# A mixture-of-experts tile stage with gate and up computed as features by tokens

## The reference

```python
router_logits = x @ gate_w.T                       # 16 experts
topk_w, topk_idx = top_k(softmax(router_logits), 4)  # 4 experts per token, weights normalised
shared = (silu(x @ Wg.T) * (x @ Wu.T)) @ shared_down.T * sigmoid(x @ shared_gate_vec.T)
for each expert e:                                 # 176 inner features
    h = silu(x @ gate_e.T) * (x @ up_e.T)
    acc = acc + (h @ down_e.T) * combine[:, e]
out = x + shared + acc
```

## Time and profile before

| what | value |
|---|---|
| median of 3 runs | 620.12 us (616.87 to 622.4) |
| profiled execution, its own time | 620.9 us |
| its span, first to last instruction | 619.1 us |
| mean granted TensorE clock | 0.986 of 2.4 GHz |
| TensorE matmul busy | 582.2 us (94%) |
| TensorE weight load busy | 457.3 us (74%) |
| VectorE busy | 492.9 us (80%) |
| ScalarE busy | 415.8 us (67%) |
| GpSimd busy | 396.7 us (64%) |

### The profile page before, as it was taken

How to read it: one execution, slowest core, us unless ns; L and a number is a source line. 1 busy time by engine, 2 the same in 40 slices (tenths; PEclk the granted TensorE clock), 3 DMA queues, 4 the chain that set the end, 5 groups by cost and what they waited for, 6 DMA issues and landing times.

```text
span 619.1 us, 18771 instructions
## 1 busy us (share of the span) xinstructions
PE 582.2 (94%) x5883; PEld 457.3 (74%) x5883; DVE 492.9 (80%) x1516; ACT 415.8 (67%) x1060; POOL 396.7 (64%) x439
## 2 busy tenths in 40 slices
PE   7789899999999999999999999978899999999991
PEld 2558779889888897898888888966467667676760
DVE  4558798989979989899878768577567789989883
ACT  4877977877868768878678586432266666666661
POOL 1147868888888878878788878696100456545553
PEclk9999999999999999999999999899899999999996
DMA  7826324334233233153202111012444677877753
GB/s 228 281 78 179 104 87 137 87 104 155 80 128 106 82 123 115 67 158 113 100 2 96 45 44 53 19 35 87 145 120 137 179 222 217 238 220 226 225 164 115
DMA packets 55682, 78.95 MB, mean 128 GB/s; under 512 B 7330, under 2 KB 46370, under 8 KB 55588
## 3 DMA queue, kind: packets, MB, share of 16 engines
q1 hardware_dynamic: 37300, 48.51, 25.9%
q0 software_dynamic: 6912, 18.88, 10.2%
q10 hardware_dynamic: 11376, 10.36, 4.9%
HBM read 44.43 MB, written 33.29 MB: 126 GB/s over the span
## 4 chain that ended last, share of the span: by engine, by line
PE 81%; POOL 6%; issue 6%; ACT 2%; DVE 2%; DMA 1%; POOLq 0%; DVEq 0%; ACTq 0%
PE ps L776 11%; PE ps L660 9%; PE ps L555 7%; PE ps L588 6%; PE ps L486 5%; PE ps L682 5%; PE ps L788 5%; PE ps L799 4%; PE ps L543 4%; PE ps L608 4%; PE ps L592 3%; PE ps L765 3%; PE ps L526 2%; POOL kv_lo L1491 2%; PE ps L516 2%
## 5 line engine op out<-in xcount | busy, mean ns | idle before, releaser
L1491 POOL TENSOR_TENSOR kv_lo<-kv,kv_hi 128x512 f16<-128x512 f32 x64 | 79.6, 1245 | 30.2 <-ACT kv_hi L914 29.9
L1562 POOL DMA_INDIRECT toeplitz_lo<-y_slots,slots x44 | 43.3, 983 | 81.3 <-DMA y_slots<-kv 57.3
L776 PE MATMUL ps<-w_gate_up_hi,toeplitz_hi 128*128 x316 | 83.6, 313 | 0.4 <-DVE toeplitz_hi L1399 0.4
L1530 POOL DMA_INDIRECT x_slots<-x_norm,slots x64 | 69.2, 1080 | 18.8 <-issue 14.4
L1479 POOL TENSOR_TENSOR kv<-ctx_t_sb,v_t 128x512 f32<-128x512 f32 x64 | 69.2, 1091 | 15.9 <-ACT v_t L903 15.8
L883 ACT ACTIVATE probs<-ps,row_neg_max 128x128 f32<-128x128 f32 x256 | 71.8, 393 | 1.1 <-DVE row_neg_max L1091 0.9
L555 PEld LDWEIGHTS ps<-v_ones,probs_t 128*128 128x128 f32 x512 | 62.2, 192 | 2.2
L555 PE MATMUL ps<-v_ones,probs_t 128*128 128x17 f32 x512 | 60.7, 256 | 0.0
L588 PE MATMUL ps<-kv_hi,toeplitz_hi 128*128 128x128 f16 x256 | 56.5, 221 | 3.2 <-POOL kv_lo L1491 1.7
L1000 ACT ACTIVATE toeplitz_hi<-ps 128x256 f16<-128x256 f32 x79 | 30.3, 384 | 43.4 <-ACT stage L1019 17.9
L588 PE MATMUL ps<-kv_lo,toeplitz_hi 128*128 128x128 f16 x256 | 56.3, 220 | 0.0
(11 more groups left out here) (226 smaller groups left out, 2074.8 us busy)
## 6 DMA issues: line engine op xcount, KB each, us to landing
stage<-in_w_units SPq DMA_DIRECT2D x36, 512.0 KB, 3.8
x_slots<-zeros SPq DMA_DIRECT2D x15, 512.0 KB
toeplitz_hi<-x_slots SPq DMA_DIRECT2D x40, 128.0 KB
y_slots<-stage ACTq DMA_DIRECT2D x40, 128.0 KB
y_slots<-kv ACTq DMA_DIRECT2D x39, 128.0 KB
kv_hi<-x_slots SPq DMA_DIRECT2D x20, 128.0 KB
x_slots<-zeros SPq DMA_DIRECT2D x1, 2432.0 KB
kv_lo<-x_slots SPq DMA_DIRECT2D x19, 128.0 KB
```

The source lines that it names most:

```text
L776: last = nc.tensor.matmul(psum[2 + t % 2][:, 0:2 * INTER], bxT[a][t % 2][:, kc, :], egu[b][:, bass.ds(e, 1), kc, :].rearrange("p a n -> p ...
L1491: nc.gpsimd.tensor_tensor(flat(kvh[1][g % 2]), kv[g % 2][:].rearrange("p h j i -> p (h j i)"), flat(kvh[0][g % 2]), ALU.subtract).then_inc ...
L1530: pool.indirect_dma_start(out=xbuf, out_offset=bass.IndirectOffsetOnAxis(ap=slots[:, row, j:j + 1], axis=0), in_=xn[2][row % 2][:], in_off ...
L1562: pool.indirect_dma_start(out=yg[n][j], out_offset=None, in_=ybuf[0:(last_tile(row, j) + 1) * P], in_offset=bass.IndirectOffsetOnAxis(ap=s ...
```

## The change

Gate and up are computed transposed. The weights of the expert are the held operand, in three chunks (112 gate, 128 made of the last 64 up and 64 gate features, 112 up), and the 128 tokens move: 3 chunks x 2 halves x 3 products = 18 matmuls of 128 columns in place of 6 of 352. The inner features then stand on the partitions, and `turn_inner` goes. ScalarE's tanh covers 256 columns in one instruction. VectorE forms (tanh + 1) x gate in two instructions of 128 columns, and the product with up in one of 256 and one of 128 columns, which write to PSUM; two of the four work across partitions 0 and 64. The down product keeps 5 matmuls, with the rows split 112 and 64. Weights are laid out anew on the host. The orders on ScalarE and VectorE are changed.

```diff
-                for kc in range(KC):
-                    for a, b, first, end in products(kc == 0, kc == KC - 1):
-                        last = nc.tensor.matmul(psum[2 + t % 2][:, 0:2 * INTER], bxT[a][t % 2][:, kc, :],
-                                                egu[b][:, bass.ds(e, 1), kc, :].rearrange("p a n -> p (a n)"),
-                                                start=first, stop=end)
+                to = psum[2 + t % 2]
+                for at, n, col in ((0, IN_A, 0), (2 * IN_A, 2 * IN_B, P), (IN_A, IN_A, 2 * P)):
+                    for kc in range(KC):
+                        for a, b, first, end in products(kc == 0, kc == KC - 1):
+                            last = nc.tensor.matmul(to[0:n, col:col + P],
+                                                    egu[b][:, bass.ds(e, 1), kc, at:at + n].rearrange("p a n -> p (a n)"),
+                                                    bxT[a][t % 2][:, kc, :], start=first, stop=end, skip_group_check=True)
...
-            def turn_inner(t):
...
-                for piece, behind in ((turn_x, 0), (gate_up, 1), (turn_inner, 2), (down_tile, 3)):
+                for piece, behind in ((turn_x, 0), (gate_up, 1), (down_tile, 3)):
...
-                nc.scalar.activation(bth[t % 2], psum[2 + t % 2][:, 0:INTER], ACT.Tanh, scale=0.5 / WS)\
-                    .then_inc(t_th.sem, 1)
+                nc.scalar.activation(bth[t % 2], psum[2 + t % 2][:, 0:E], ACT.Tanh, scale=0.5 / WS).then_inc(t_th.sem, 1)
...
-                for piece, behind in ((x_hi, 0), (gate_th, 1), (inner_hi_tile, 2), (y_out, 3)):
+                for piece, behind in ((x_hi, 0), (inner_hi_tile, 2), (gate_th, 1), (y_out, 3)):
...
+            def inner_tile(t):
...
+                t_th.wait(dve, t)
+                to, g, sg = psum[4 + t % 2], psum[2 + t % 2], bsg[t % 2]
+                nc.vector.scalar_tensor_tensor(out=sg[0:IN_B, 0:P], in0=bth[t % 2][IN_B:P, P:2 * P], scalar=1.0,
+                                               in1=g[IN_B:P, P:2 * P], op0=ALU.add, op1=ALU.mult)
+                nc.vector.scalar_tensor_tensor(out=sg[0:IN_A, P:2 * P], in0=bth[t % 2][0:IN_A, 0:P], scalar=1.0,
+                                               in1=g[0:IN_A, 0:P], op0=ALU.add, op1=ALU.mult).then_inc(t_sg.sem, 1)
+                t_sg.wait(dve, t)
+                t_hlo.wait(dve, t - 2)
+                nc.vector.scalar_tensor_tensor(out=to[0:IN_A, 0:2 * P], in0=g[0:IN_A, P:3 * P], scalar=SILU,
+                                               in1=sg[0:IN_A, :], op0=ALU.mult, op1=ALU.mult).then_inc(t_in.sem, 1)
+                t_in.wait(dve, t)
+                nc.vector.scalar_tensor_tensor(out=to[IN_B:P, 0:P], in0=g[0:IN_B, P:2 * P], scalar=SILU,
+                                               in1=sg[0:IN_B, 0:P], op0=ALU.mult, op1=ALU.mult).then_inc(t_inner.sem, 1)
...
-                for piece, behind in ((x_lo, 0), (gate_tile, 1), (inner_lo_tile, 2)):
+                for piece, behind in ((x_lo, 0), (inner_lo_tile, 2), (inner_tile, 1)):
```

More of the change, by code:

```diff
@@ L21 @@
 EXPERTS, TOP, INTER, SHARED = 16, 4, 176, 704
+IN_A, IN_B = 112, 64
 NB = 16
@@ L251, in build @@
         acc = [st[:, 1024 + n * E:1024 + (n + 1) * E] for n in range(2)] + [z_mem[:, TOP * E:(TOP + 1) * E]]
-        bth = [st[:, 1536 + n * INTER:1536 + (n + 1) * INTER] for n in range(2)]
-        bga = [st[:, 1888 + n * INTER:1888 + (n + 1) * INTER] for n in range(2)]
-        bhh = [st[:, 2240 + n * E:2240 + (n + 1) * E] for n in range(2)]
+        bsg = [st[:, 2240 + n * E:2240 + (n + 1) * E] for n in range(2)]
+        bth = [st[:, 1536 + n * E:1536 + (n + 1) * E] for n in range(2)]
         psum = [stack.enter_context(nc.psum_tensor(f"ps{n}", [P, 512], F32)) for n in range(8)]
@@ L303, in build @@
         down_done, xsh_ready = signal("down_done"), signal("x_shared_ready")
+        s_set = sem("buffers_set")
         s_tab_pe = sem("table_products")
@@ L315, in build @@
         t_xT, t_xhi, t_xlo = signal("tile_x_transposed"), signal("tile_x_hi"), signal("tile_x_lo")
-        t_gu, t_th, t_ga, t_inner = (signal(f"tile_{n}") for n in ("gate_up", "tanh", "gated", "inner"))
-        t_hT, t_hhi, t_hlo = signal("tile_inner_transposed"), signal("tile_inner_hi"), signal("tile_inner_lo")
+        t_gu, t_th, t_in, t_inner = (signal(f"tile_{n}") for n in ("gate_up", "tanh", "inner", "inner_twice"))
+        t_sg = signal("tile_gated")
+        t_hhi, t_hlo = signal("tile_inner_hi"), signal("tile_inner_lo")
         t_dn, t_y = signal("tile_down"), signal("tile_y")
@@ L773, in gate_up @@
                 e = experts[t]
-                for kc in range(KC):
-                    for a, b, first, end in products(kc == 0, kc == KC - 1):
-                        last = nc.tensor.matmul(psum[2 + t % 2][:, 0:2 * INTER], bxT[a][t % 2][:, kc, :],
-                                                egu[b][:, bass.ds(e, 1), kc, :].rearrange("p a n -> p (a n)"),
-                                                start=first, stop=end)
-                last.then_inc(t_gu.sem, 1)
-            def turn_inner(t):
[L782 to L789, removed]
+                to = psum[2 + t % 2]
[5 more added lines that the diff above has]
+                                                    bxT[a][t % 2][:, kc, :], start=first, stop=end, skip_group_check=True)
+                last.then_inc(t_gu.sem, 1)
             def down_tile(t):
@@ L798, in down_tile @@
                 for a, b, first, _ in products(True, False):
-                    nc.tensor.matmul(to, bhT[a][t % 2][:, 0, :], eda[b][:, bass.ds(e, 1), :].rearrange("p a n -> p (a n)"),
-                                     start=first, stop=False)
-                nc.tensor.matmul(to, bhT[0][t % 2][:, 1, :], edb[:, bass.ds(e, 1), :].rearrange("p a n -> p (a n)"),
+                    nc.tensor.matmul(to, bhT[a][t % 2][0:IN_A, 1, :],
+                                     eda[b][0:IN_A, bass.ds(e, 1), :].rearrange("p a n -> p (a n)"), start=first, stop=False)
+                nc.tensor.matmul(to, bhT[0][t % 2][:, 0, :], edb[:, bass.ds(e, 1), :].rearrange("p a n -> p (a n)"),
                                  start=False, stop=False)
-                nc.tensor.matmul(to, bhT[1][t % 2][:, 1, :], edb[:, bass.ds(e, 1), :].rearrange("p a n -> p (a n)"),
+                nc.tensor.matmul(to, bhT[1][t % 2][0:IN_B, 0, :],
+                                 edb[0:IN_B, bass.ds(e, 1), :].rearrange("p a n -> p (a n)"),
                                  start=False, stop=True).then_inc(t_dn.sem, 1)
             for s in range(TILES + 3):
-                for piece, behind in ((turn_x, 0), (gate_up, 1), (turn_inner, 2), (down_tile, 3)):
+                for piece, behind in ((turn_x, 0), (gate_up, 1), (down_tile, 3)):
                     if 0 <= s - behind < TILES:
@@ L1004, in gate_th @@
                 t_gu.wait(act, t)
-                t_ga.wait(act, t - 2)
-                nc.scalar.activation(bth[t % 2], psum[2 + t % 2][:, 0:INTER], ACT.Tanh, scale=0.5 / WS)\
-                    .then_inc(t_th.sem, 1)
+                t_sg.wait(act, t - 2)
+                nc.scalar.activation(bth[t % 2], psum[2 + t % 2][:, 0:E], ACT.Tanh, scale=0.5 / WS).then_inc(t_th.sem, 1)
             def inner_hi_tile(t):
-                t_hT.wait(act, t)
+                t_inner.wait(act, t)
                 t_dn.wait(act, t - 2)
@@ L1333, in _ @@
             table_after = {"ix": round_tiles, "hl1": mark_tiles, "fin": copy_table}
-            s_set = sem("buffers_set")
             for n in range(2):
@@ L1390, in _ @@
             for n in range(2):
-                nc.vector.memset(bhh[n][:, P:], 0.0).then_inc(s_set, 1)
+                nc.vector.memset(bsg[n][:, 0:P], 0.0).then_inc(s_set, 1)
             dve.wait_ge(s_set, 14)
@@ L1400, in x_lo @@
                                         bxT[0][t % 2].rearrange("p c n -> p (c n)"), ALU.subtract).then_inc(t_xlo.sem, 1)
-            def gate_tile(t):
+            def inner_tile(t):
+                if t < 2:
+                    for use, _ in BANKS[4 + t]:
+                        READER[use][0].wait(dve, NB - 1, READER[use][1])
                 t_th.wait(dve, t)
[L1404 to L1413, removed]
+                to, g, sg = psum[4 + t % 2], psum[2 + t % 2], bsg[t % 2]
[10 more added lines that the diff above has]
+                                               in1=sg[0:IN_B, 0:P], op0=ALU.mult, op1=ALU.mult).then_inc(t_inner.sem, 1)
             def inner_lo_tile(t):
@@ L1633, in weight_units @@
     units += list(down.reshape(2, 3, P, E).transpose(0, 2, 1, 3))
-    egu = a["L0_ffn_expert_gate_up"].reshape(EXPERTS, 2 * INTER, KC, P).transpose(0, 3, 2, 1)
+    gate, up = np.split(a["L0_ffn_expert_gate_up"], 2, axis=1)
+    egu = np.concatenate([gate[:, :IN_A], up[:, :IN_A], up[:, IN_A:], gate[:, IN_A:]], axis=1)
+    egu = egu.reshape(EXPERTS, 2 * INTER, KC, P).transpose(0, 3, 2, 1)
     units += list(egu)
     ed = a["L0_ffn_expert_down"].transpose(2, 0, 1)
[L1637 to L1640, removed]
```

(4 more changed lines are left out.)

## The result

The changed kernel takes 713.46 us (median of 4 runs, 710.67 to 716.33) against 619.05 us for the kernel before: a ratio of 1.1525, 95% interval 1.1469 to 1.1581. The forecast was 685 us, with a range from 650 to 705. The slowdown was forecast, and two thirds of its size (64 of 94 us); the rest was not.

The account below looks back on a forecast made before the run. TensorE's queue and array were both taken to need about 2.0 us a step; the queue's +0.94 - 0.13 = +0.81 us over 79 steps gave +64 us on 620.9, so 685 us, range 650 to 705.

Parts of the forecast that it names:

- What bounds the kernel: Tile stage of the kernel before: TensorE's array and its instruction queue both take about 2.0 us of the 2.045 us step.
- Added in the queue: Gate and up in TensorE's queue: two more blocks of six pairs with four address steps, +0.94 us a step (0.8 to 1.0).
- the removed part: turn_inner leaving TensorE's queue, one wait and two pairs of weight load and matmul: 0.13 us a step saved (0.05 to 0.2).
- The long index loads ... stay as they are, being in the queue: Index loads of up to 600 ns in TensorE's queue: expected unchanged, adding nothing to the step.
- The sum: TensorE's queue per step: +0.94 - 0.13 = +0.81 us, so 2.045 becomes 2.86 us; over 79 steps +64 us, 685 us.
- Slow weight loads: Rival: 112-column weight loads at 0.106 us make the array decide, step 2.66 us, 670 us (662 at 93 ns); 14%.
- The estimate of 93 ns apiece: Gate and up's 112-column weight loads, by the Trainium skill's formula: about 93 ns each, making the array's block 1.46 us.
- the array would wait for its queue during the whole block: Gate and up: the array's 1.01 us is less than the queue's 1.41, so nothing is stored up at the index load.
- The down product stays at 0.55 us: Down product in TensorE's array: still five matmuls of 256 columns, 0.55 us a step.
- VectorE: Rival: VectorE decides with 2.08 us a step, 2.5 with a combine, mean 2.41; +29 us, 650 us; 12%.
- A longer queue: Rival: dynamic weight loads cost more to issue, or more code is fetched; block +1.2 us, +1.07 a step, 706 us; 13%.
- Drain, ScalarE, the new waits: Last tile's drain, ScalarE's wider tanh (under 0.1 us a step, hidden) and VectorE's new wait on itself: each put at nothing.

Follow-up runs that it names:

- b_multi_nc: Kernel before with four experts' indices read by one load in every fourth step, ahead of gate and up, without range checks: 609.74 us, ratio 0.985.
- b_split: Kernel before with each of the six gate and up matmuls issued in three pieces of 112, 128 and 112 columns: 712.78 us, ratio 1.150.
- a_early: Changed kernel with the index load moved from behind gate and up to in front of it: 685.77 us, ratio 1.110.
- a_half_early: Changed kernel with the index load in front of gate and up and 64 of 128 tokens moving there from the third tile on: 707.08 us, ratio 1.143.
- a_sp_late: Changed kernel with only SyncE's tile load issue moved behind the index load, ScalarE's store issue left ahead of it: 697.95 us, ratio 1.128.
- a_act_late: Changed kernel with only ScalarE's store issue moved behind the index load, SyncE's tile load issue left ahead of it: 682.31 us, ratio 1.103.
- b_early: Kernel before with the index load moved in front of gate and up, still one load for each tile: 624.72 us, ratio 1.008.
- b_load_last: Kernel before with the index load moved to the end of the step, behind the down product: 631.23 us, ratio 1.024.

## Why the prediction was wrong

**What bounds the kernel** (right). Queue and array together at about 2.0 us a step: relieving the queue alone brings 1.5% (`b_multi_nc`), 9 us where that run's expectation, from 1.9 us of array work, said 10. Tripling the block's instructions alone costs 93 us (`b_split`), 17 of them by the longer index load.

**Added in the queue** (right). +0.94 us a step forecast; the block takes a median of 1.47 instead of 0.47 us, and `b_split` shows 0.98. What is left of `a_early`'s +0.84 a step makes the removed part about 0.15, and 0.13 was forecast. The form, 6 FUSED_REGOPS and 6 ALU_OP a tile, came as said.

**"The long index loads ... stay as they are, being in the queue"** (the step that failed). The sum took the load's time as a constant, 0.324 us in the mean and 0.301 in the median. It became 0.676 and 0.714. The longer block carried the load from a place ahead of ScalarE's store issue to 0.7 us behind it, and a load there returns only about 1.45 us (median) after that issue. 0.35 us x 79 = 28 us, which is the gap between 685 and 713. With the store moved (682, 684 us) or the load (686 us) the forecast holds. The trace of before had the sign of it: loads up to 600 ns, which I named and did not ask about. Without the first load, 8 of the 9 slow ones start 1.0 to 1.3 us behind a store of the output by SyncE. In the prediction's own terms, the term for the index load was put at no change because the load sits in TensorE's queue; what it lacked is the place in time that the load takes relative to the other engines' stores.

**Slow weight loads** (rival, fell). The 112-column loads show 130 ns each against 98 for 128 columns, but their matmuls follow each other by 0.055 us like the others:

```profile
602.54 0.22 PE L780 MATMUL ps<-toeplitz_hi,w_gate_up_lo 128*112 128x128 f16 x1
602.54 0.19 PEld L780 LDWEIGHTS ps<-toeplitz_hi,w_gate_up_hi 128*112 x2
602.60 0.28 PE L780 MATMUL ps<-toeplitz_hi,w_gate_up_hi 128*112 128x128 f16 x2
602.65 0.13 PEld L780 LDWEIGHTS ps<-toeplitz_hi,w_gate_up_lo 128*112 x1
602.71 0.22 PE L780 MATMUL ps<-toeplitz_hi,w_gate_up_lo 128*112 128x128 f16 x1
```

The estimate of 93 ns apiece, from the Trainium skill ("TensorE: Matmul & The Clock Gate", the rule in Weight-path perf modes, the formula in LDWEIGHTS), does not hold as the cost in this stream: the measurement is 0.055 us. That a load of 112 columns is slower by itself agrees with the rows (130 against 98 ns); here it is hidden. I had also said that the array would wait for its queue during the whole block. It does not: the queue gains a lead under the down product's long matmuls (its first FUSED_REGOPS is at 601.9, the first matmul at 602.49) and spends it in the block.

**The down product stays at 0.55 us** (wrong, without effect on the time). Its last matmul has 64 rows now, and from its first matmul (604.74) to the transposes behind it (605.49) it takes 0.75 us. The array had that much to spare, as it waited for its queue.

**VectorE** (right as a rival for steps with a combine, 2.5 against 2.46 us; by the terms shown, 2.08 + 0.47, it is 2.55). That its 650 us meets 647 and 650 is partly luck: the steps without a combine were put at 2.08 us and take 2.30. With 2.46 and 2.07 us, 55 and 23 steps of each, VectorE alone would still take 2.35 us a step (an estimate from these rows) and make the change a loss.

**A longer queue** (rival; near in its time, 706 against 713, by luck and not by its cause). The dispatch of a dynamic weight load costs what a dynamic matmul costs: `b_split` and the changed kernel share their 474 + 474 register instructions and their block of 1.5 us. The range ended at 705, just under this rival's own time, so that the chance of lying outside it was larger than the 15% stated.

**Drain, ScalarE, the new waits** at nothing: nothing in the runs speaks against it, since `a_early` meets the sum's step, 2.88 against 2.86 us; none was tested by itself.

What stays open is why a load from SBUF into a register has to wait behind a store's issue. The runs show when it returns and that the tile load alone doesn't cause it, not what the two share.

## What to carry to other kernels

When an engine is busy all the time, read its queue's small instructions too: here six matmuls with their four address steps take 0.47 us of queue, whatever they move. That is less than their 0.89 us of array with 352 columns, but more than the 0.33 us (6 x 0.055) with 128. When a change lengthens one engine's part of a step, list what slides past what on the other queues, and treat the outliers of a duration (600 among 300 ns) as a warning that it depends on its neighbours. Here a register load was worth batching over four iterations without a check for each value (610 us), and not with the checks (633 us); leaving them out supposes that the values are safe.

## What the runs showed of the hardware

- A TENSOR_LOAD from SBUF takes 0.30 us, and mostly 0.4 to 0.8 us where a DMA store was issued 0.6 to 1.1 us before (74 of 79 loads over 0.35 us in the changed kernel); at the low clock of `a_half_early` most that start 0.6 us behind one are not lengthened. A lengthened load returns a median of 1.2 us behind the issue (`a_sp_late`), 1.45 with SyncE's load issued beside it. A load that starts under 0.5 us behind a store (`a_act_late`) or 1.3 us and more behind it (`b_early`, `b_load_last`) takes 0.30 to 0.35. One that fetches four values takes 0.33 us undisturbed.
- With 64 instead of 128 columns in 18 of 25 matmuls of each step, the granted clock was 0.50 from 449 us on, against 1.00 with all columns, and the kernel 21 us slower for half the arithmetic of the block.
- 112-column fp16 weight loads do not slow a stream of 128-column matmuls at 2.4 GHz: 0.055 us each.
- The down product's last matmul, with 64 rows, starts 0.21 us behind its predecessor (128 rows) and the transposes 0.21 us behind it, where these distances were 0.11 us in the kernel before. The number of rows is the only difference of form; no run tested it by itself:

```profile
605.07 0.27 PE L795 MATMUL ps<-w_down_rest,toeplitz_hi 128*128 x1
...
605.28 0.28 PE L797 MATMUL ps<-w_down_rest,toeplitz_hi 64*128 x1
...
605.49 0.44 PE L767 MATMUL ps<-identity,toeplitz_hi 128*128 128x128 f32 x2
```
